# Attention stage reordered, gates of tokens 128 to 511 as row products, idle-time identity products on TensorE

## The reference

```python
x = x + matmul(fake_quant(_layernorm(x), s1, z1), fake_quant(ctx, s2, z2))   # (2,512,1024) x (2,1024,1024)
h = _layernorm(x)
vision_len = int(512 * 0.3)
modality_ratio = mean(abs(h[:, vision_len:])) / (mean(abs(h[:, :vision_len])) + 1e-8)   # one per batch
gate_scores = softmax(concat([h, modality_ratio]) @ gate_w + gate_b)         # 3 experts
top_val, top_idx = top_k(gate_scores, 2); top_val = top_val / (sum(top_val) + 1e-8)
for i in range(2):
    j = top_idx[:, 0, i]                      # the batch's FIRST token chooses
    moe_out = moe_out + top_val[..., i:i + 1] * (act_j(h @ w1[j] + b1[j]) @ w2[j] + b2[j])
x = x + moe_out
```

## Time and profile before

| | us |
|---|---|
| runs | 398.29, 399.26, 399.35; median 399.26 |
| the profiled execution, span | 398.3 |
| TensorE busy in it | 384.2 (96%) |
| DVE busy | 319.4 (80%) |
| ACT busy | 194.6 (49%) |
| POOL busy | 75.4 (19%) |

### The profile page before, as it was taken

One profiled execution on the slowest core, in us unless ns is written; L12 is line 12 of the kernel. 1 busy time (PEld: TensorE's weight loads), 2 busy tenths in 40 slices (PEclk: granted clock), 3 DMA queues, 4 the chain that ended last, 5 costly groups with the idle time before them and its releaser, 6 DMA issues.

```text
span 398.3 us, 5246 instructions
## 1 busy us (share of the span) xinstructions
PE 384.2 (96%) x1860; PEld 302.7 (76%) x1860; DVE 319.4 (80%) x529; ACT 194.6 (49%) x253; POOL 75.4 (19%) x94
## 2 busy tenths in 40 slices
PE   1999999999999999999999999999999999999996
PEld 1345656888888888888888888888888888888885
DVE  8689967999599799898899995654997864639972
ACT  3477745274247635372755833344475244424720
POOL 8647500352110001063103001030000010110000
PEclk9999999999999999999999999999999999999999
DMA  8997019719654676728002898965065884550112
GB/s 300 412 410 305 3 50 375 264 21 282 121 105 137 233 229 226 180 39 158 15 0 90 304 291 281 248 118 96 0 209 172 262 275 88 105 106 2 53 53 107
DMA packets 27437, 66.98 MB, mean 168 GB/s; under 512 B 2160, under 2 KB 2192, under 8 KB 27280
## 3 DMA queue, kind: packets, MB, share of 16 engines
q1 hardware_dynamic: 23888, 54.01, 38.8%
q0 software_dynamic: 3456, 12.58, 16.5%
q10 hardware_dynamic: 64, 0.02, 0.0%
HBM read 49.83 MB, written 4.19 MB: 136 GB/s over the span
## 4 chain that ended last, share of the span: by engine, by line
PE 89%; DVE 6%; POOL 1%; issue 1%; ACT 1%; POOLq 0%; ACTq 0%
PE ps L1655 44%; PE ps L1623 38%; PE ps L1415 4%; DVE bn L840 2%; DVE xres L911 2%; PE ps L1449 1%; POOL ctxq L453 1%; PE ps L1403 1%; DVE hT_lo L920 0%; DVE ctxq L858 0%; POOL ctxq L446 0%; DVE q L874 0%; POOL q_rstd L427 0%; DVE q_bias L1147 0%; PE ps L1484 0%
## 5 line engine op out<-in xcount | busy, mean ns | idle before, releaser
L1037 DVE TENSOR_TENSOR w_lo<-raw,w_hi 128x1024 fp32r<-128x1024 f32 x88 | 103.4, 1218 | 2.6 <-ACT w_hi L688 2.4
L688 ACT ACTIVATE w_hi<-raw 128x1024 fp32r<-128x1024 f32 x88 | 87.8, 1052 | 34.5 <-DVE raw L1050 18.0
L1655 PE MATMUL ps<-hT_hi,w_hi 128*128 128x512 f32 x256 | 100.0, 391 | 0.0
L1655 PE MATMUL ps<-hT_lo,w_hi 128*128 128x512 f32 x256 | 99.6, 389 | 0.0
L1655 PE MATMUL ps<-hT_hi,w_lo 128*128 128x512 f32 x256 | 99.6, 389 | 0.0
L1623 PE MATMUL ps<-w_hi,a_hi 128*128 128x512 f32 x224 | 87.4, 390 | 0.0
L1623 PE MATMUL ps<-w_hi,a_lo 128*128 128x512 f32 x224 | 87.2, 389 | 0.0
L1623 PE MATMUL ps<-w_lo,a_hi 128*128 128x512 f32 x224 | 87.1, 389 | 0.0
L776 ACT ACTIVATE act_f<-ps,b1T 128x512 f32<-128x512 f32 x32 | 22.1, 689 | 112.4 <-PE ps L1655 112.4
L523 POOL DMA_DIRECT2D raw<-raw x24 | 21.3, 1038 | 193.0 <-DMA raw<-in_L_ffn_w_dram 137.9
L1655 PEld LDWEIGHTS ps<-hT_hi,w_hi 128*128 128x128 f32 x256 | 48.1, 188 | 10.6 <-issue 0.4
(11 more groups left out here) (155 smaller groups left out, 367.9 us busy)
## 6 DMA issues: line engine op xcount, KB each, us to landing
raw<-in_L_ffn_w_dram SPq DMA_DIRECT2D x64, 512.0 KB, 5.2
raw<-raw POOLq DMA_DIRECT2D x24, 512.0 KB, 6.6
raw<-in_ctx_dram SPq DMA_DIRECT2D x16, 512.0 KB, 11.8
xres<-in_x_dram SPq DMA_DIRECT2D x8, 512.0 KB, 9.7
out_dram<-xres SPq DMA_DIRECT2D x16, 256.0 KB, 4.1
b2row<-in_L_ffn_b_dram SPq DMA_DIRECT2D x4, 512.0 KB, 6.0
gate_rows<-in_L_ffn_gate_w_dram SPq DMA_DIRECT2D x1, 1536.0 KB, 17.7
small<-in_L_xattn_x_scale_dram ACTq DMA_DIRECT2D x2, 0.0 KB
```

The lines of the kernel that those rows point to most:

```text
L688: nc.scalar.activation(w_hi[n % SLOTS][:, 2 * c:2 * c + 2, :], region(q)[:, 2 * c:2 * c + 2, :], ACT.Copy).then_inc(w_hi_ready, 1)
L1037: V.tensor_tensor(w_lo[n % SLOTS][:, 2 * c:2 * c + 2, :], region(n % QUARTERS)[:, 2 * c:2 * c + 2, :], w_hi[n % SLOTS][:, 2 * c:2 * c + 2, ...
L1655: last = T.matmul(ps[:, G1_BANK + f % 2, :], w[q % SLOTS][:, k % TT, fs], h[:, k, :], start=n == 0, stop=n == 3 * KT - 1)
```

## The change

- **Tables and banks.** Other engines code other tiles: DVE codes one context tile (7) for two (2 and 4) and one x tile for two, ACT h tile 2. All PSUM bank numbers of the stage change, and the waits for a free bank with them.
- **Order.** The first stage is written in another order on TensorE, DVE, ACT and POOL. Row sums of batch 0 come before most of its column sums; `turn_bias` goes to the start.
- **Gate.** TensorE makes logits for tile 0 of batch 0 alone (`gate_product(0, 0)`, a turn of one product for four). `choose_experts` takes the first tile's scores only. The gates of the other three tiles come from `gate_dot` on DVE in the first pass (9), and for batch 1 tile 0 in the second (3) and the others in the third (9). `gate_values` moves into the first and the third pass.
- **Bias rows.** `bias_add` of passes 0 and 1 both stand in pass 1, of passes 2 and 3 in pass 3; in those passes `b2row` is loaded behind w2, and only once the earlier row's four adds are done.
- **Identity products.** `keep_busy(n)` issues n products of 128 columns of two constants into bank 5, which nothing reads then: 34 + 30 + 8 + 10 + 24 = 106.

```diff
+DOTS_BEFORE = [NE * (TT - 1), NE * TT, NE * (2 * TT - 1)]
+FIRST, OTHERS = slice(0, 1), slice(1, TT)
+WARM_BANK = 5
+WARM_FIRST = 34
+WARM_NEXT = 30
+WARM_GAP = 8
+WARM_WAIT = 10
+WARM_LAST = 24
...
+            def load_b2(p, e):
+                if p:
+                    sp.wait_ge(b2_used, TT * p)
+                if p == TOP_K:
+                    sp.wait_ge(hT_ps, B * TT)
+                sp.dma_start(b2row[:], b2[bass.ds(e, 1), :].to_broadcast([P, D])).then_inc(b2_in, 16)
...
-                if p:
-                    sp.wait_ge(b2_used, TT * p)
-                if p == TOP_K:
-                    sp.wait_ge(hT_ps, B * TT)
-                sp.dma_start(b2row[:], b2[bass.ds(e, 1), :].to_broadcast([P, D])).then_inc(b2_in, 16)
+                if p % TOP_K == 0:
+                    load_b2(p, e)
                 load_w1(p, 2, e)
                 load_w1(p, 3, e)
                 for q in range(4):
                     load_w2(p, q, e)
+                if p % TOP_K:
+                    load_b2(p, e)
...
+            def keep_busy(n):
+                for _ in range(n):
+                    T.matmul(ps[:, WARM_BANK, 0:P], ident_b[:], ones_b[:], start=True, stop=True)
+
             pe.wait_ge(const_ready, 7)
+            keep_busy(WARM_FIRST)
             pe.wait_ge(scales_in, 16 * 4)
             T.matmul(ps[:, CONST_BANK, 0:4], ones[0:1, :], small[0:1, 0:4], start=True, stop=True
                      ).then_inc(scales_ps, 1)
+            keep_busy(WARM_NEXT)
             turn_gate_weights()
+            keep_busy(WARM_GAP)
             transpose_q1(0)
+            keep_busy(WARM_WAIT)
             transpose_q1(1)
+            turn_bias()
+            keep_busy(WARM_LAST)
```

More of the change, by code:

```diff
@@ L514, in _ @@
             h_tile(3)
+            quant_ctx(13)
             x_rstd(6, 2)
-            quant_x(6)
-            for t in range(TT):
-                h_power(TT + t)
-                h_offset(TT + t)
+            quant_ctx(15)
+            quant_x(7)
             def add_regions(into, other, done):
@@ L546, in _ @@
             t4_sum(0)
+            for t in range(TT):
+                h_power(TT + t)
+                h_offset(TT + t)
             t3_sum(1)
@@ L965, in turned_scores, with dot_scores @@
                 dve.wait_ge(logit_ps, 1)
-                lps = ps[:, TURN_BANK[0], 0:4 * TT].rearrange("p (t e) -> p e t", e=4)
+                lps = ps[:, TURN_BANK[0], 0:4]
                 for e in range(NE):
-                    last = V.tensor_scalar(sc[:, e, :], lps[:, e, :], gbias[:, e:e + 1], None, ALU.add)
+                    last = V.tensor_scalar(sc[:, e, FIRST], lps[:, e:e + 1], gbias[:, e:e + 1], None, ALU.add)
                 then(last)
-            def dot_scores():
-                dve.wait_ge(dots_done, NE * TT)
-                dve.wait_ge(h_rstd_ready, B * TT)
+            def dot_scores(b, cols):
+                first, end = b * TT + cols.start, b * TT + cols.stop
+                dve.wait_ge(dots_done, NE * (end - 1))
+                dve.wait_ge(h_rstd_ready, end)
@@ L975, in dot_scores @@
                 for e in range(NE):
-                    last = V.tensor_tensor(dot[:, e, :], dot[:, e, :], h_rstd[:, TT:B * TT], ALU.mult)
+                    last = V.tensor_tensor(dot[:, e, cols], dot[:, e, cols], h_rstd[:, first:end], ALU.mult)
                 then(last)
                 for e in range(NE):
-                    last = V.tensor_scalar(sc[:, e, :], dot[:, e, :], gbias[:, e:e + 1], None, ALU.add)
+                    last = V.tensor_scalar(sc[:, e, cols], dot[:, e, cols], gbias[:, e:e + 1], None, ALU.add)
@@ L1256, in _ @@
                             s4_sum(p, k - 1)
-                    if f == 0:
-                        if p > 0:
-                            w_lo_quarter(q + 3)
-                        else:
-                            pass
+                    if f == 0 and p > 0:
+                        w_lo_quarter(q + 3)
                     elif f == 2 and p == 0:
@@ L1359, in wait_attn_bank @@
             def wait_attn_bank(b, t):
-                if (b, t) == (0, 2):
-                    for i in range(TT):
-                        wait_q1T(pe, i)
+                if (b, t) == (0, 0):
+                    pe.wait_ge(gw_ready, 1)
                 elif (b, t) == (0, 3):
@@ L1588, in _ @@
+            transpose_q1(6)
             column_sums(1, 6)
+            transpose_q1(7)
+            codes_product(1, 1, 7)
+            gate_turn()
+            codes_product(1, 0, 7)
+            row_sums(1)
             codes_product(1, 2, 0)
+            codes_product(1, 2, 6)
             codes_product(1, 2, 1)
+            codes_product(1, 2, 7)
+            codes_product(1, 3, 0)
+            codes_product(1, 2, 5)
             codes_product(1, 2, 2)
+            add_terms(1, 0)
+            codes_product(1, 3, 4)
```

496 lines of the change are left out of this document (246 added, 250 removed).

## The result

The changed kernel takes 395.42 us (median of 4 runs, 394.77 to 395.59) against 399.31 us (4 runs) for the kernel before, a ratio of 0.9904 with a 95% interval of 0.9891 to 0.9918. Forecast were 394.8 us and a range of 393.2 to 398.0. The profiled execution has a span of 393.8 us, which is the forecast's 398.3 - 4.5 to the tenth; that it agrees so well is partly luck, as the rest shows: the choice came 0.7 us later than forecast, the way from it to the first activation was 1.2 us shorter, and the second pass lost 0.9 us where 0.3 were booked.

A forecast was written before the change was run, and what follows sets the result against it. The kernel was taken as a first stage, ended by the first expert's choice, plus a fixed 328.2 us on TensorE. Choice 4.8 us earlier less 0.3 us stall gives 4.5: 399.26 - 4.5 = 394.8 us, range 393.2 to 398.0.

The forecast's parts named there:

- first codes product: TensorE's start: codes products begin at about 13.1 us instead of 12.07, behind the identity products, at full pace.
- first `attn_add`: DVE, first stage: starts at 24.5 us, 3.4 us earlier than 27.88.
- first expert written: DVE's choice of the first expert: at 50.7 us against 55.47, a gain of 4.8 us.
- w2 part of the second pass: Second pass: TensorE's own work hides DVE's changed load; only a 0.3 us stall is booked for the pass.
- Up to the choice: First stage to first expert: full pace, last context tile on DVE, one-tile logits; choice 4.8 us earlier.
- From the choice to the first activation: 14.6 us of w1 loading and rounding stay unchanged; only the choice sets the activation, microsecond for microsecond.
- The new wait: Second pass: second `b2row` loads near 158 us, lands 6.0 us later; TensorE's transpose near 174 stalls 0 to 1.7, booked 0.3.
- the slower case: Rival, second pass: `b2row` lands late behind w2, TensorE waits; at 12 us the time is 401.5 us; chance 0.05.
- What the passes pay: DVE: first pass about nothing on 72.5 of 82 us, third rises to 71, second loses 1; TensorE hides all.
- The clock: TensorE's start: identity products lift the pace early, 512-column products take 0.22 us; at worst first transpose 0.8 us later.
- The meeting of DVE and POOL: Near 14 us: DVE's `quant_x(2)` meets POOL's context-tile coding, may cost 0.9 us more; counted as nothing.
- The anchor: Profile to time: the runs' median lies 1.0 us above the profiled execution of 398.3 us, so 399.26 - 4.5 = 394.8.

The follow-up runs named there:

- a_gate4: The changed kernel, but TensorE again makes the gate logits of all four tiles of batch 0 ahead of the first choice; 400.75 us.
- a_pe_late: The changed kernel with 18 more identity products (1.0 us) on TensorE ahead of the first product with w1; 395.62 us.
- d_pe_late: a_dots with 18 more identity products (1.0 us) on TensorE ahead of the first product with w1; 395.49 us.
- d_split: a_dots with DVE's column split of batch 1 moved behind the choice of experts; 394.81 us.
- a_dots: The changed kernel with batch 1 tile 0's three row products moved into earlier DVE waits of the second pass; 394.98 us.
- a_choice_late: The changed kernel with five dependent small DVE steps, about 1.0 us, ahead of the first choice of experts; 396.60 us.
- a_nofill: The changed kernel without its 106 identity products; 396.35 us.
- b_fill: The kernel before with the same 34 + 30 + 8 + 10 + 24 identity products in its start; 399.09 us.
- b_shift: The kernel before with 34 products of 8 columns added at TensorE's start; 398.75 us.
- d_fetch: a_dots with the first 34 identity products of 128 columns made 68 of 64 columns; 394.96 us.

## Why the prediction was right, step by step

| step | forecast | measured |
|---|---|---|
| first codes product | 13.1 at full pace | 13.10, full pace |
| last column sums of batch 0 | 20.8 | 21.5 |
| first `attn_add` | 24.5 | 25.18 |
| first expert written | 50.7 | 51.41 |
| first activation | 65.3 | 64.81 |
| second `b2row` issued, wait on TensorE | 158.0, 0.3 us | 157.94, none |
| w2 part of the second pass | hidden | + 0.89 us |
| end of the span | 393.8 | 393.8 |

**Up to the choice** the step that failed is the last context tile, which DVE began at 19.89 and I had at 19.6, with 0.4 us of product and queue behind it. From the first add to the expert I had 26.2 us and it took 26.2. The gain on the choice was 4.06 us, not 4.8.

**From the choice to the first activation** I had 14.6 us "that the change leaves as they are", and it took 13.4. This was the wrong step. I took a first block 0.55 us longer than the third one as a sign that weights alone set the activation. In the kernel before TensorE started its first product with w1 at 64.08 without waiting for weights, behind its own batch 1 work; only the 0.55 us in the block came from weights, 0.3 of it from the late chunk. So the activation at 70.12 was set by TensorE's queue as much as by the choice. TensorE's queue became 5.0 us earlier too; a_gate4 shows that most of this comes from the same removal of gate products, copy and turns that made the choice earlier, and so the sum came out close. That a microsecond on the choice is one on the end, "and nothing else in the stage is", was wrong: a_pe_late, d_pe_late and d_split show the two paths within 0.3 us of each other after the change.

**The new wait** of the second pass, which carried the slower case, came out as sketched, and at the transpose that I watched it cost nothing:

```profile
157.94 0.34 SPq L362 DMA_DIRECT2D b2row<-in_L_ffn_b_dram  x1
...
161.78 2.48 DVE L1128 SCALAR_TENSOR_TENSOR xres<-b2row,gate,xres 128x1024 f32<-128x1024 f32 x2 [1.81 <-DMA b2row<-in_L_ffn_b_dram]
...
168.96 3.40 POOL L487 TENSOR_SCALAR b2row<-xres,h_rstd,h_shift 128x1024 f32<-128x1024 f32 x1
...
173.41 1.03 PE L1491 MATMUL ps<-ident,b2row 128*128 128x128 f32 x8
```

The row was issued at 157.94 and its first adds started 3.8 us later, POOL's tile was written by 172.36, and TensorE transposed it at 173.41, 1 us later and without a wait. By these rows a load of 6.0 us, 2.2 more than here, would have met this 1 us of slack with a stall of about 1 us; that is an estimate. The wait did cost something where I did not look: its 1.81 us on DVE are missing at the end of the pass, and a_dots won the 0.89 us back in part by filling it with a row product.

**What the passes pay** was right for the third pass (71.6 us of DVE for 71), 2.7 us too low for the first (75.2 where I had it unchanged at 72.5), which TensorE did not feel, and missed the second. I had looked at its DVE sum (1 us less than before) and not at its place: eight bias adds and the statistics of three tiles stand early now, and three row products late, from 178.86 us, just ahead of the w2 part in which DVE was already at 45.6 of 49 us. That, with the row and the meeting above, cost 0.89 us where I had 0.3 for a stall at the transpose.

**The clock.** The level rose at 6.6 us, as the forecast wanted, and by 8.1 us in nine other profiles with filler. But this is not certain in each execution: in the profile of a_choice_late a small DMA came later, TensorE stood idle for 0.79 us, and the second 30 identity products ran at the slow pace, then in the way of the gate weights:

```profile
6.79 0.59 PE L1550 MATMUL ps<-small,ones 1*128 1x4 f32 x2 [0.79 <-DMA small<-in_L_xattn_x_zp_dram]
7.31 3.30 PE L1545 MATMUL ps<-ones_b,ident_b 128*128 128x128 f16 x30
...
14.71 1.46 PE L1455 MATMUL ps<-ctxq,q1T 128*128 128x512 f16 x6
```

Codes began at 14.71 there, 1.6 us late. I had priced this at 0.8 us "at worst". It is one of four executions of that kernel by its times (398.0, against 396.2 to 397.0).

The rule that I cited from the Trainium skill, TensorE: Matmul & The Clock Gate, section "What's actually happening" (slow by default, lifted by activity), agrees with what the filler did: 0.107 us a product, then 0.056 from 6.6 us on, against a rise near 17.4 us without filler.

**The meeting of DVE and POOL** near 14 us, which I had counted as nothing, hardly took place: `quant_x(2)` took 0.81 us and was over at 14.54, and POOL's tile began at 14.43. A small step of DVE beside that tile took 0.76 us for some 0.15, and DVE's wait of 1.92 us for the last context tile took this up. The same meeting in the second pass, which I had not looked for, cost DVE 2.0 us. The Trainium skill, SBUF — State Buffer, section "Who interferes with whom", has the later one of the two blocked for a whole instruction. The rows of a_nofill roughly agree: DVE's product of 1.59 us starts 0.52 us after POOL's tile and ends 1.41 us behind its end. In the changed kernel the length agrees (2.0 us more, beside a tile of 1.84), but not the order: DVE's row starts 0.28 us ahead of POOL's, and it is DVE that takes longer. Why is open.

**The anchor.** I put the median 1.0 us above the profiled execution. By the 12 experiments a time is 1.7 us above its span, so the profile of before was one of its slower executions (about 400.0, where its runs lie from 397.9 to 400.9), and the gain between medians is 3.9 us where that between spans is 4.5. The excess probably lies in the first stage: from the first product with w1 to the end this profile has 334.2 us, those of b_fill and b_shift, which run the same passes, 334.2 and 333.8. So the 5.1 us by which w1 starts earlier are some 0.6 too many for a middling execution. That, and not a step of the sum, is most of the 0.6 us between 394.8 and 395.4.

## What to carry to other kernels

Before a step that sets an end is made earlier, write down what the next engine's own queue would do without it; where it starts without waiting, both paths count, and a gain needs both. Early filler pays only in an order that can use the pace: the same products were worth 0.9 us in one order and nothing that could be told in the other. Work moved "to where it is hidden" is to be judged by the busy share of the stretch it lands in, not of the pass: DVE at 45.6 of 49 us had no room for three row products of 1.6 us and a wait for a late row, and moving them to its waits of 3.0 and 1.8 us gave 0.9 us of the span back (0.4 of the median).

## What the hardware showed

- A 16 KB packet of the instruction queue kept one DMA engine busy for 1.0 us, and in the three executions in which it fell among the landings of the first four 512 KB loads of w1 one of them was 1.2 to 1.4 us late; in the eleven others none was late by more than 0.5 us. The packet moved when instructions were added to TensorE at its start, some 50 us earlier than the loads (from 62 to 49 us in b_shift, from 66 to 64 in d_fetch).
- 34 products of only 8 columns at the start (b_shift) were followed by a faster start of the codes products, 5.41 us for 18 against 6.50. The profile does not tell whether they caused it.
- A DVE step of 0.43 us took up to 2.47 us (d_pe_late) beside a POOL tile of 1.84 us.
